# Issuing the expert gathers and scatters one by one in the first half of a step instead of four in a row in its second half

## What is computed

```python
x = x + tanh(g_xattn[0]) * xattn0(layernorm(x), ctx, mask0)      # 16 heads of 16, 77 keys
x = x + tanh(g_ffn[0])   * moe(layernorm(x))                     # layer 0: 8 experts, top 2
x = x + tanh(g_xattn[1]) * xattn1(layernorm(x), ctx, ctx, mask1)
x = x + tanh(g_ffn[1])   * fourier(layernorm(x))                 # one real 256x256 product + bias

# moe: logits = h @ gate_w.T; the two best experts of each token, weights from a softmax
# each expert: (up * gelu(gate)) @ down, 256 -> 2 x 1024 -> 256; the two results are mixed
```

## Time and profile before

| | before |
|---|---|
| runs | 1343.78, 1349.95, 1759.76 us (median 1349.95) |
| profiled execution | 1340.18 us |
| its span | 1338.6 us, mean granted clock 0.944 |
| PE busy | 1210.1 us (90%) |
| DVE busy | 890.7 us (67%) |
| ACT busy | 570.9 us (43%) |
| POOL busy | 261.6 us (20%) |

### The profile page before, as it was taken

How to read it: one execution, slowest core, us unless ns; L and a number is a source line. 1 busy time by engine, 2 the same in 40 slices (tenths; PEclk the granted TensorE clock), 3 DMA queues, 4 the chain that set the end, 5 groups by cost and what they waited for, 6 DMA issues and landing times.

```text
span 1338.6 us, 35030 instructions
## 1 busy us (share of the span) xinstructions
PE 1210.1 (90%) x11816; PEld 1001.9 (75%) x11816; DVE 890.7 (67%) x2695; ACT 570.9 (43%) x1187; POOL 261.6 (20%) x374
## 2 busy tenths in 40 slices
PE   4898999988869999899998999999997999999996
PEld 3777777777658888688886888888874777777784
DVE  4787767777647675565856676766565777777763
ACT  4565555545423232422324242422233555555462
POOL 5024334233320000000000000000022334433310
PEclk9998978878779999999999999999997999999998
DMA  9544324334434021131301212101122222222200
GB/s 294 169 129 145 125 89 139 105 113 152 153 127 147 32 92 59 48 105 36 126 31 59 95 56 88 40 29 37 39 65 66 64 72 87 77 75 70 86 29 24
DMA packets 82755, 119.67 MB, mean 89 GB/s; under 512 B 27325, under 2 KB 52557, under 8 KB 80588
## 3 DMA queue, kind: packets, MB, share of 16 engines
q1 hardware_dynamic: 64172, 60.32, 14.6%
q0 software_dynamic: 12848, 49.05, 11.2%
q10 hardware_dynamic: 5616, 8.78, 1.8%
HBM read 63.81 MB, written 47.58 MB: 83 GB/s over the span
## 4 chain that ended last, share of the span: by engine, by line
PE 77%; DVE 8%; issue 7%; ACT 2%; SPq 2%; ACTq 2%; DMA 1%; POOL 0%; DVEq 0%; POOLq 0%; another core or an unknown queue 0%
PE bank L1758 25%; PE bank L1771 13%; PE bank L1519 7%; PE bank L1585 7%; PE bank L1441 5%; PE bank L1572 3%; PE bank L1504 3%; PE bank L1502 3%; PE bank L1461 3%; PE bank L1525 2%; PE bank L1596 1%; PE bank L1545 1%; PE bank L1583 1%; DVE bm L1081 1%; PE bank L1487 1%
## 5 line engine op out<-in xcount | busy, mean ns | idle before, releaser
L1758 PE MATMUL bank<-tiles,we 128*128 128x256 f16 (+1 forms) x3744 | 395.3, 259 | 5.9 <-issue 5.0
L1758 PEld LDWEIGHTS bank<-tiles,we 128*128 128x128 f16 x3744 | 326.1, 98 | 47.5 <-issue 13.5
L935 ACT ACTIVATE tiles<-bank 128x256 f32<-128x256 f32 (+1 forms) x312 | 109.5, 354 | 336.0 <-PE bank L1758 302.5
L1771 PE MATMUL bank<-we,tiles 128*128 128x256 f16 x1608 | 224.8, 274 | 20.9 <-DVE tiles L1372 20.0
L1368 DVE SCALAR_TENSOR_TENSOR tiles<-bank,tiles 128x256 f32<-128x256 f32 (+1 forms) x312 | 120.1, 385 | 165.7 <-ACT tiles L935 161.6
L1771 PEld LDWEIGHTS bank<-we,tiles 128*128 128x128 f16 x1608 | 148.2, 98 | 58.3 <-DVE tiles L1372 33.7
L1081 DVE TENSOR_REDUCE bm<-bank 128x4 bf16<-128x308 f32 x256 | 116.5, 475 | 78.7 <-PE bank L1504 62.9
L1519 PE MATMUL bank<-qT,kbd 128*128 128x256 f16 x960 | 166.7, 294 | 2.4 <-issue 1.4
L471 DVE TENSOR_TENSOR pr<-pr 128x512 f16<-128x512 f32 x160 | 108.5, 682 | 35.2 <-ACT pr L797 32.7
L1374 DVE TENSOR_TENSOR tiles<-tiles 128x256 f16<-128x256 f32 (+1 forms) x312 | 121.1, 388 | 12.1 <-DVE tiles L1372 1.7
L1519 PEld LDWEIGHTS bank<-qT,kbd 128*128 128x128 f16 x960 | 99.1, 106 | 24.8 <-issue 3.0
(11 more groups left out here) (197 smaller groups left out, 1693.3 us busy)
## 6 DMA issues: line engine op xcount, KB each, us to landing
expert_out<-zeros SPq DMA_DIRECT2D x16, 896.0 KB
wes<-in_guT POOLq DMA_DIRECT2D x9, 1024.0 KB, 5.1
tiles<-expert_in SPq DMA_DIRECT2D x29, 256.0 KB, 2.6
pr<-in_guT POOLq DMA_DIRECT2D x7, 1024.0 KB
yg<-in_dnT POOLq DMA_DIRECT2D x7, 1024.0 KB
expert_out<-tiles ACTq DMA_DIRECT2D x28, 256.0 KB, 2.1
expert_in<-zeros POOLq DMA_DIRECT2D x8, 640.0 KB, 12.8
xin<-in_x SPq DMA_DIRECT2D x16, 256.0 KB
```

The lines of the kernel that those rows point to most:

```text
L935: act.activation(ge[:, fc % 2, 0:n * P], bank[1 + fc % 3][:, 0:n * P], ACT.Gelu, scale=INV).then_inc(s.gelu, 1)
L1758: last = pe.matmul(bank[1 + fc % 3][:, half * S:half * S + w * P], gate_up[:, par, c, i, col:col + P], xT[:, j, c, 0:w * P], start=n == 0, ...
L1771: last = pe.matmul(bank[4 + t][:, 0:D], act16[:, fc % 4, i, t * P:(t + 1) * P], we[:, par, 2, j, fc * D:(fc + 1) * D], start=fc == 0 and n ...
```

## The change

The four indirect DMAs of a batch are issued apart, earlier in the step. With `one(n)` for the n-th of the four, POOL's step becomes: wait for `mask_ready` of the step (so the first scores of b run), `one(0)`; wait for `attended_high` of b-1 (ACT has copied the transposed attended rows, and the output projection starts), `one(1)` and `one(2)`; `ln_root(1, b-1)`; `one(3)`; `root(b+2)`.

In layer 0 the scatters of a step are now those of b-3 instead of b-2, from step 3 on; step 15 issues those of b-2 too, and the last two batches follow the loop as before. In layer 1 the gathers are still those of b+3, and `recall` runs one step further ahead (b+4, now before `normalise` and not at the head of the step), so that the slots are there at the step's start; `slots` has one more, unused entry for it.

```diff
             def step(b, front, tail, pre, ld):
...
-                late = b.layer == 0 and not (isinstance(b.i, int) and b.i < 2)
+                late = b.layer == 0 and not (isinstance(b.i, int) and b.i < 3)
+                part = ld and b.layer == 1
+                one = (lambda n: gather(b.after(3), n)) if part else (lambda n: scatter(b.after(-3), n))
+                if part:
+                    wait_apart(pool, s.places_recalled, b.i + 4)
+                if late:
+                    scatter_ready(b.after(-3))
+                if late or part:
+                    wait_apart(pool, s.mask_ready, b.n + 1)
+                    one(0)
+                    if tail:
+                        wait_apart(pool, s.attended_high, pv.n + 1)
+                    one(1)
+                    one(2)
                 if tail:
                     ln_root(1, s.root_after, s.variance_after, pv)
+                if late or part:
+                    one(3)
                 if pre:
                     root(b.after(2))
-                if ld and b.layer == 1:
-                    gather(b.after(3))
-                if late:
-                    for t in range(QT):
-                        scatter(b.after(-2), t)
+                if b.layer == 0 and isinstance(b.i, int) and b.i == 15:
+                    scatter_ready(b.after(-2))
+                    for n in range(2 * QT):
+                        scatter(b.after(-2), n)
...
             def step(b, front, tail, pre, ld):
                 nx, pv = b.after(1), b.after(-1)
-                if ld and b.layer == 1:
-                    recall(b.after(3))
...
+                if ld and b.layer == 1:
+                    recall(b.after(4))
                 normalise(b)
```

53 lines of the change are left out of this document (27 added, 26 removed).

## The result

| | before | changed |
|---|---|---|
| median of 20 runs, us | 1345.78 | 1335.02 |
| lowest to highest, us | 1335.16 to 1353.02, one run at 1759.76 | 1326.64 to 1337.35 |
| ratio, 95% interval | | 0.9912, 0.9896 to 0.9927 |
| span of the profiled execution, us | 1338.6 | 1328.8 |

The account below looks back on a forecast made before the run. PE ends the chain in 77% of the span, and indirect DMAs delay its small matmuls. Gains of 13.2 + 1.6 + 22.5 + 1.0 = 38.3 from 1340.2 give 1301.9; plus 3 for measured runs, 1305 us, range 1280 to 1344.

Parts of the forecast that it names:

- layer-0 sum: Steps 3 to 13 of layer 0: 15.1 + 3.2 = 18.3 us a step, a gain of 2.05 x 11 = 22.5 us.
- the landing of `one(3)`: Layer 0's fourth scatter, issued 10.6 us into the step, lands 2.4 us later, so `h2_norm` starts at 13.0.
- The place of the lag: Four indirect DMAs cost a step about 1.65 us beside small matmuls, next to nothing beside matmuls 256 columns wide.
- What layer 1 keeps: Twelve layer-1 steps: `one(3)` keeps 0.55 of the 1.65 us loss, leaving a gain of 1.10 x 12 = 13.2 us.
- The tail of 5.3 us: Layer 0, from the second norm's start at 13.0 to the step's end at 18.3, with 3.20 us from `tail_out` on.
- the first rival: Layer 0's clock stays up, gaining a further 1.4 us a step, 15 us in all: 1290 us; chance 0.13.
- 1 us of gain on all of it: Step 2, step 15 and the last batches' scatters together gain 1 us, a rounding.
- Slower: Early DMAs delay the front chain from attended rows to `h2_norm`; at 1.15 us each, 31 us lost: 1371 us; chance 0.11.
- The DMAs are not the cause: Missing statistics and norm for b+2 explain the 1.65 us; nothing moves in layer 1: 1340 to 1343 us; chance 0.09.
- The clock stays up: Layer 0: a shorter second half keeps full clock, so the wide front part gains 1.4 us a step: 1290; chance 0.13.
- the relief: Layer 0 from `tail_out` to the step's end: 3.20 us instead of 5.00, within a step gain of 2.05 us.

Follow-up runs that it names:

- `ahead_clear_2`: `ahead_mixed` with the 896 KB clear of the expert output moved behind `spread`, on a chip with the lag; 1272.21 us, ratio 0.9439 to the kernel before.
- `all_early`: `ahead_fetch` with the 896 KB clear of the expert output moved behind `spread`, on a chip with the lag; 1263.70 us, ratio 0.9455 to the kernel before.
- `l1_only_2`: Layer 1 as in the changed kernel, layer 0 as in the kernel before, on a chip with the lag; 1313.28 us in one run.
- `two_late`: The changed kernel with layer 1's third and fourth gather back behind the root for b+2, on a chip without the lag; 1328.79 us in one run.
- `clear_late`: The changed kernel with SP's 896 KB clear of the expert output moved behind `spread`, on a chip without the lag; 1278.16 us in one run.
- `ahead_mixed`: The changed kernel with layer 0's fourth scatter ahead of the second norm's root, and the old order in steps 14 and 15; 1255.62 us, ratio 1.0013.
- `lag_twice`: The kernel before with idle VectorE reductions, two per layer-0 step and one per layer-1 step, on a chip with the lag; 1368.72 us.
- `ahead_fetch`: The changed kernel with layer 0's fourth scatter ahead of the root, and steps 14 and 15's weights wait and fetch behind scatters and roots; 1262.34 us, ratio 1.0080.

## Why the prediction was right and wrong

*The step that failed is the layer-0 sum.* It gave a step of 18.3 us, a gain of 22.5 us over steps 3 to 13; the step took 21.4, a loss of 11.3. Two of its terms were mis-sized, the landing of `one(3)` and the tail behind it, and steps 14 and 15 had no term of their own. Layer 1 gained more than its term. One by one:

*The place of the lag: right on chips that have it.* The prediction read from rows 3 to 7 that four indirect DMAs cost some 1.65 us beside small matmuls in ping-pong and next to nothing beside wide ones. On chips with the lag that holds in four programs (the changed kernel, `ahead_clear_2`, `all_early`, `l1_only_2`); on the others they cost next to nothing at either place.

*What layer 1 keeps: wrong size.* I left 0.55 us a step for `one(3)`. Next to nothing stays: 17.37 us a step against 17.22 without gathers, and 17.33 in the old order on a chip without lag. So `one(3)` does not keep a quarter of the loss. Whether because it is a single one or because it is issued at 9.1 us into the step, 2.6 us ahead of the first gather before, was not separated: `two_late` was to tell it and came to a chip without lag. The term was 13.2 us and measured 21.9; with the first step and its neighbours nearer 24 (`l1_only_2`).

*The landing of `one(3)`: the term that failed first.* I took 2.4 us between bounds of 2.3 and 3.3, both from stretches where nothing else was on the way. Over the eleven steps the second norm starts on average 4.2 us behind the issue (9.8 us in, norm at 14.0). The cause stood in the code and in the trace: SP issues 1.7 MB from 6.9 to 9.0 us into the step, so the engines are full when this one transfer must get through. `clear_late` shows it: with the clear out of the way the landing takes 2.56 us. The Trainium skill, "DMA: Bandwidth & Descriptors", Anatomy of one DMA, has 2.0 us + bytes/436 GB/s, which gives an estimate of 2.3 us here. The traces come near it while the engines are nearly free (2.56 us) and not beside a full set (4.05).

*The tail of 5.3 us: right at full clock, wrong here.* The prediction let the step end 3.20 us behind `tail_out`, the price of step 1, read at full clock. The longer wait leaves TensorE idle before the thin part (2.31 us against 0.82) and the clock falls to 1.2 GHz inside the tail: 7.4 us on average, against 5.41 in `clear_late`. The prediction had said that PE would idle there, but used it only against the first rival and not against its own sum. Together, against 10.6, 2.4 and 5.3: issue 0.8 earlier, landing 1.8 later, tail 2.1 longer, 3.1 us over the 18.3 forecast, and 21.4 measured.

*Steps 14 and 15: left out.* "I put 1 us of gain on all of it, a rounding." They lost 9.3. Before, GpSimd's wait for the expert's weights stood ahead of a short root; now three DMAs and their issue stand between it and the root, and the fourth, issued at 11.2 us into step 14, lands 5.6 us later, with the 1 MB fetch on the engines as well. `ahead_mixed`, with the old order in these steps, takes 16.11 and 14.77 us for them.

*The sum.* With the measured terms (layer 1, the step behind it and the stretch ahead of it -28, steps 2 to 13 +9, steps 14 and 15 +9) it is the measured -10. The direction was right because one layer gained more than the other lost. That is luck: the forecast had both layers gaining, two errors of opposite sign met, and on a chip without the lag the same change is slower.

*The rivals.* "Slower" priced early DMAs on the front chain; in `ahead_clear_2`, with four early scatters, that chain is not late: the norm starts at 9.5 to 10.0 us in nine of the ten steps, as without lag. "The DMAs are not the cause" and the rule named beside it (the Trainium skill, "SBUF — State Buffer", Who interferes with whom, by which a DMA never holds up a compute engine and TensorE and ScalarE wait for no one) agree with the chips without lag; on the one where it was measured the gathers cost 0.05 us a step. On the others the forecast drawn from them, no gain from moving the DMAs, fails by 1.65 us a step in layer 1 and about 4 in layer 0. The rule speaks of ports, and no run here shows by which way the lateness comes. "The clock stays up" did not come with this change, but with `one(3)` mended it does, in all of steps 3 to 12, and the step falls from 20.35 to 16.33 us: 2.05 of it is the relief that the sum already had; the other 2 I put down to the clock, where I gave it 1.4, though no run measured the two apart.

*What was not foreseeable from the trace of before.* That a fifth of its layer-0 and a tenth of its layer-1 step are absent from the same program on other chips. On a chip without the lag the same change is 6% slower. Open: what the lag is, whether it stays with a chip from session to session, and whether two lags of the measured length would by themselves put layer 0 at half clock; `ahead_clear_2` shows only that both come and go with the scatters' place.

## What to carry to other kernels

Price the landing of a small DMA by what is on the engines when it is issued, not by its landing elsewhere: one scatter behind 1.7 MB took 4.2 us instead of 2.6, and the step behind the longer wait took 2 us more, part of it at the lower clock. Put a transfer that somebody will wait for ahead of the step's big ones or of the chain that waits, and move a bulk clear that nobody waits for out of its way; on chips with the lag that turned -0.9% into -5.5%. And when a profile shows idle time with no cause in the program, measure the kernel on more chips before changing it: the same change was worth -0.9% on one and +6.0% on another.

## What the runs showed of the hardware

- The same program takes 1250 to 1256 us on four chips and 1333 to 1353 us on the others. The difference begins 0.8 us behind the issue of the first scatter beside small matmuls, before the second is issued: DVE and ACT go on 1.2 and 1.55 us late, both behind PE, while POOL issues on time.
- The lag does not add to other waiting: with an idle reduction of 1.91 us at its place a layer-1 step takes 18.9 to 19.1 us with gathers and 18.86 without (`lag_twice`).
- Where the second norm waited 3.56 us, TensorE fell to its lower level (granted 0.69 over the rest of the step, 7.01 us); where it waited 2.07 us it stayed at the full 2.4 GHz (1.00, 5.41 us).
- A scatter of 128 rows lands in 2.56 us with the DMA engines nearly free, in 4.05 us behind a set at share 1.02, and in step 14 of `ahead_fetch`, with the engines at share 1.04, in 6.2.
